# Moving the attention of a Macaron block against its mixture-of-experts passes, by a table of times

## The chip, the cores and the metric

The kernel runs on one NeuronCore of a Trainium2 chip. The metric is device time in microseconds (us), from the first to the last instruction of one launch. Engines: PE is TensorE, DVE is VectorE, ACT is ScalarE, POOL is GpSimd, SP is SyncE, which here only issues DMAs. Each engine works through its own instructions in a fixed order and waits on semaphores for the others.

## The reference

Eight batches (B) of 512 tokens (S) with 256 features (D) go through three sublayers:

```python
x = x + 0.5 * ffn(layernorm(x))          # "first" pass of the batch
x = x + attn(layernorm(x))               # RMS norm inside, 16 heads of 16, causal, output projection, + residual
x = x + 0.5 * ffn(layernorm(x))          # "second" pass of the batch

def ffn(x):                              # top-1 of E = 2 experts, FF = 1024
    probs = softmax(x @ gate_w.T); sel = argmax(probs); top_w = probs[sel]
    h = silu(x @ w_gate[sel].T) * (x @ w_up[sel].T)
    return (h @ w_down[sel].T) * top_w
```

`attn` is `softmax(mask(q k^T / 16)) v @ Wo + residual` with q, k, v from `rms_norm(x) * rms_w`.

## The kernel before, in words

**The FFN.** Tokens of one or two batches are sorted by expert into one array in DRAM (`x_sorted`) and processed in slots of 128 tokens. There are 12 passes (`PASSES`): 8 of one batch (5 slots) and 4 of two batches (9 slots), 76 slots in all. In a pass's first and last slot the expert is known when the program is built; in those between, the address of the weights is computed in registers (`expert[n, s]`, L1072 and L1080). A slot has two units (halves of FF). A unit is `gate` and `up` on PE (24 matmuls each, L1135 to L1137), `tanh` on ACT (L737), `hid` on DVE (L946, L950), the split into a high and a low part (`h_split`: L743 on ACT, L676 on POOL), and `down` on PE (12 matmuls, L1154 to L1156).

**The route of a batch** leads up to its pass: statistics on DVE (`l_stats`, L897), scale on POOL (L603 to L606), the normed rows on ACT (`l_norm`, L716; `l_split`, L724, which waits until the batch before has been scattered, L723), the low part on POOL (`l_low`, L610), the router's logits on DVE (`l_dlogit`), a count of places on PE (`l_prefix`, L1099 to L1104), the places on DVE (`l_pos`, L931), the scatter by four indirect DMAs from POOL (`l_scatter`, L624), and the transposed load from SP (`l_load`, L518) that the pass's first `gate` waits for (L1124). Behind a pass, POOL gathers the rows back (`y_gather`, L649, four indirect DMAs) and adds them to x (`x_update`, L631).

**Attention.** For each batch: `stats` on DVE (L957, waits for `x_update`), `rstd` on POOL, `norm` on ACT (L768), two `transpose` stages (PE L1169, ACT L778, DVE L975), `residual` on DVE, six projections (`proj`: PE L1060, then ACT L796 or L788, then DVE), and for q and k a store to DRAM (`qk_store`) from which SP reads the heads back in another layout (`qk_in`, eight DMAs a part). Then four parts of four heads (32 parts in all). A part has ten fills: `scores` on PE (L1197, L1199), `row_min` on DVE; later, from the row maxima on, `scores_t` on PE (L1214, L1216), `exp` on ACT (L814, L815), `p_lo` on DVE (L1029) for eight fills and on POOL (L681) for two, `pv` on PE (L1234), and `o_norm` on DVE. When the four parts are done come two transposes ("o") and two `out_proj`. `scores`, `scores_t`, transposes and projections take turns in three PSUM banks.

**What sets the order.** `master()` gives every stage a point on one common axis and sorts; every engine runs its share in that order. An FFN slot is 12 points and the passes stand at fixed points (`PASS_AT`, the last one ending at 925). Attention part p starts at `PART_AT + PART_POINTS * p`; a batch's norm, projections and loads stand at fixed distances ahead of its first part. A point has no fixed length: the engines take what time they need, and wait where the order lets them run into each other.

Of the kernel before, what the change touches and what calls it, by code (L numbers as in the profile page):

```python
# [33 lines left out]
GROUPS = 4  # L34
# [75 lines left out]
UNIT_POINTS = 6  # L110
SLOT_POINTS = 2 * UNIT_POINTS
PASS_AT = [SLOT_POINTS * at for at in SLOT_AT[:4]] + [336, 396, 462, 522, 630, 738, 798, 865]
PART_AT = 115
PART_POINTS = 21
FILL_POINTS = PART_POINTS / 10
LEAD = 33
PAIR_LAG = 9

NORM_AT = [-40, -39.5, -38.5, -36, -34, -32.4]
RESIDUAL_AT = -33  # L120
PROJ_AT = [-30.7, -28.2, -25.7, -23.2, -20.7, -18.2]
STORE_LAG = 1.0
QK_IN_AT = [-22, -16, -14, -14]
MAX_PARTS_AT = 21.5
ROW_MAX_AT = 24
SOFTMAX_AT = 31
# [5 lines left out]
COEF_LAG = 1.0  # L132
GATHER_LAG = 8
UPDATE_LAG = 16
OUT_AT = [122, 123.5, 125.5, 127.5]
ROUTE_STEPS = [("l_stats", 0, 0.0), ("l_stats", 1, 0.5), ("l_rstd", 0, 1.5), ("l_norm", 0, 4.0),
               ("l_split", 0, 6.0), ("l_dlogit", 0, 6.0), ("l_low", 0, 8.5), ("l_exp", 0, 10.5), ("l_prefix", 0, 11.0),
               ("l_pos", 0, 11.2), ("l_coef", 0, 13.0), ("l_scatter", 0, 14.5), ("l_load", 0, 19.0)]
# [9 lines left out]
def part_at(p, point):  # L148
    return PART_AT + PART_POINTS * p + point


def master():

    plan = []

    def put(at, *stage):
        plan.append((at, len(plan), stage))

    for u, (n, s, q) in enumerate(UNITS):
        p = PASS_AT[n] + SLOT_POINTS * s + UNIT_POINTS * q  # L160
        if s == 0 and q == 1:
            put(p, "flags", n)
            put(p + COEF_LAG, "coef", n)
        for kb in range(KB):
            put(p + kb, "gate", u, kb)
            put(p + 2 + kb, "up", u, kb)
            put(p + 10 + kb, "down", u, kb)
        put(p + 1 + TANH_LAG, "tanh", u)
        put(p + 3 + HID_LAG, "hid", u)
        put(p + 5.5, "h_split", u)  # L170
        if q:
            put(p + 11.3, "y_out", u // 2)
            put(p + 12.3, "y_store", u // 2)

    for k, (n, i, what, b) in enumerate(ITEMS):
        end = PASS_AT[n] + SLOT_POINTS * SLOTS[n] + 5.2 * i
        put(end + GATHER_LAG, "y_gather", k)
        at = end + UPDATE_LAG
        if what == "first":
            at = min(at, part_at(GROUPS * b, NORM_AT[0]) - 1)  # L180
        put(at, "x_update", k)
        at = PASS_AT[n] - LEAD - PAIR_LAG * (len(PASSES[n]) - 1 - i)
        if what == "second":
            at = max(at, part_at(GROUPS * b, OUT_AT[3] + 1))
        elif b >= 2:
            put(at - 8, "x_load", b)
        for stage, part, off in ROUTE_STEPS:
            if stage == "l_load":
                if i == len(PASSES[n]) - 1:
                    put(START_AT[stage, part] if n == 0 else at + off, stage, n)  # L190
            else:
                put(START_AT[stage, part] if n == 0 else at + off, stage, k, part)

    for w, at in enumerate(MAX_AT):
        put(at, "w_max", w)
    for k, at in enumerate(SCALE_AT):
        put(at, "w_scale", k)
    for w in range(PIECES):
        put(SPLIT_AT[w], "w_split", w)
    put(UNIT_POINTS * ONES_UNIT + 5.6, "ones")  # L200

    for b in range(B):
        first = GROUPS * b
        norm = [("stats", b, 0), ("stats", b, 1), ("rstd", b), ("norm", b), ("transpose", b, "attn", 0),
                ("transpose", b, "attn", 1)]
        for where, stage in zip(NORM_AT, norm):
            put(part_at(first, where), *stage)
        put(part_at(first, RESIDUAL_AT), "residual", b)
        for m in range(NP):
            put(part_at(first, PROJ_AT[m]), "proj", b, m)  # L210
            put(part_at(first, PROJ_AT[m] + STORE_LAG), "qk_store", b, m)
        out = [("transpose", b, "o", 0), ("transpose", b, "o", 1), ("out_proj", b, 0), ("out_proj", b, 1)]
        for where, stage in zip(OUT_AT, out):
            put(part_at(first, where), *stage)

    for p in range(PARTS):
        put(part_at(p, QK_IN_AT[p % GROUPS]), "qk_in", p)
        for f in range(FILLS):
            put(part_at(p, f * FILL_POINTS), "scores", p, f)
            put(part_at(p, f * FILL_POINTS) + ROW_MIN_LAG, "row_min", p, f)  # L220
            at = part_at(p, SOFTMAX_AT + (f + 0.5) * FILL_POINTS)
            put(at, "scores_t", p, f)
            put(at + EXP_LAG, "exp", p, f)
            put(at + FILL_POINTS, "p_lo", p, f)
            put(at + PV_LAG * FILL_POINTS - 0.2, "pv", p, f)
            if f % KINDS == KINDS - 1:
                put(at + PV_LAG * FILL_POINTS + 0.8, "o_norm", p, f // KINDS)
        put(part_at(p, MAX_PARTS_AT), "max_parts", p)
        put(part_at(p, ROW_MAX_AT), "row_max", p)

    return [stage for _, _, stage in sorted(plan)]
# [13 lines left out]
def macaron(nc, x, rms_w, gate_w, w_gate, w_up, w_down, w_attn, out):  # L245
    with ExitStack() as ctx:  # L246
# [1036 lines left out]
```

## Time and profile before

| | us |
|---|---|
| median of 3 runs (1254.82 to 1256.56) | 1255.71 |
| the profiled execution | 1255.95 |
| its span, first to last instruction | 1254.2 |

| engine | busy us | share |
|---|---|---|
| PE | 1078.9 | 86% |
| DVE | 860.2 | 69% |
| ACT | 744.7 | 59% |
| POOL | 571.8 | 46% |

PE's busy time is a union of pipelined matmuls. Idle time before an instruction is shown in brackets with what ended it.

### The profile page before, as it was taken

What the parts mean: (1) busy time and instruction counts of PE and PEld (TensorE: products, weight loads), DVE (VectorE), ACT (ScalarE), POOL (GpSimd) and SP (SyncE); (2) the same over time, 40 slices, a digit from 0 to 9 for tenths busy, and PEclk for the clock granted to TensorE, in tenths of its full rate; (3) what the DMA queues carried; (4) which work ended last, traced back from release to release, by engine and by line L of the source; (5) the groups of instructions that cost most, each with busy time, mean ns of one, the idle gap of its engine ahead of it and who ended that gap; (6) DMA issues with size and microseconds to landing.
All of it is one profiled execution on the core that took longest, in us unless ns stands there. A gap on an engine that the chain in (4) does not pass through costs nothing. (4 is left out here: it accounts for less than half of the span.)

```text
span 1254.2 us, 39207 instructions
## 1 busy us (share of the span) xinstructions
PE 1078.9 (86%) x14566; PEld 933.9 (74%) x14566; DVE 860.2 (69%) x1784; ACT 744.7 (59%) x1285; POOL 571.8 (46%) x693
## 2 busy tenths in 40 slices
PE   0677889986979989989998799998999999989894
PEld 0666778775868877778777678877777888778774
DVE  6643646785767886767787867888677797775421
ACT  3532525674757866666676667775766676776321
POOL 3146544344352344645354545334573255655443
PEclk9889889997989999989999899999999999999998
DMA  8203251212211122122223041112321112211211
GB/s 316 84 24 90 66 94 45 78 45 81 59 53 48 32 63 75 47 64 64 80 60 94 25 112 53 41 33 70 81 81 36 53 33 73 84 50 49 53 44 47
DMA packets 110670, 83.99 MB, mean 67 GB/s; under 512 B 59616, under 2 KB 104416, under 8 KB 110496
## 3 DMA queue, kind: packets, MB, share of 16 engines
q1 hardware_dynamic: 93408, 54.22, 15.7%
q0 software_dynamic: 6144, 17.31, 4.3%
q10 hardware_dynamic: 10944, 9.97, 2.5%
q8 instruction: 131, 2.15, 0.7%
q14 instruction: 43, 0.35, 0.1%
HBM read 37.26 MB, written 34.23 MB: 57 GB/s over the span
## 5 line engine op out<-in xcount | busy, mean ns | idle before, releaser
L676 POOL TENSOR_TENSOR h_lo<-hid,h_hi 128x256 bf16<-128x256 f32 x304 | 217.7, 737 | 480.9 <-ACT h_hi L743 479.9
L814 ACT ACTIVATE area<-ps_w,s_scale 128x512 f32<-128x512 f32 x320 | 219.4, 686 | 218.0 <-PE ps_w L1216 170.1
L1135 PE MATMUL ps_g<-x_t,w 128*128 128x128 f16 x1096 | 209.8, 226 | 15.5 <-issue 9.2
L1029 DVE TENSOR_TENSOR area<-area 128x512 f16<-128x512 f32 x256 | 206.6, 807 | 18.9 <-ACT area L815 15.4
L815 ACT ACTIVATE area<-ps_w,s_scale 128x512 f16<-128x512 f32 x320 | 218.0, 681 | 0.0
L1137 PE MATMUL ps_g<-x_t,w 128*128 128x128 f16 x1096 | 209.9, 226 | 2.0 <-issue 1.8
L1136 PE MATMUL ps_g<-x_t,w 128*128 128x128 f16 x1096 | 209.1, 225 | 1.8 <-issue 1.8
L1135 PE MATMUL ps_u<-x_t,w 128*128 128x128 f16 x1096 | 205.6, 222 | 2.9 <-issue 2.7
L1137 PE MATMUL ps_u<-x_t,w 128*128 128x128 f16 x1096 | 205.8, 222 | 1.7 <-issue 1.5
L1136 PE MATMUL ps_u<-x_t,w 128*128 128x128 f16 x1096 | 204.5, 221 | 1.8 <-issue 1.8
L1154 PE MATMUL ps_y<-wd,h_hi 128*128 (+1 forms) x608 | 169.1, 278 | 14.8 <-POOL h_lo L676 12.1
L1156 PE MATMUL ps_y<-wd,h_lo 128*128 (+1 forms) x608 | 169.2, 278 | 0.3 <-issue 0.3
L1155 PE MATMUL ps_y<-wd,h_hi 128*128 (+1 forms) x608 | 169.0, 278 | 0.1
L1197 PE MATMUL ps_w<-kt,qt 65*128 65x512 f16 (+3 forms) x512 | 138.2, 308 | 17.9 <-DVE row_min L1006 11.8
L1214 PE MATMUL ps_w<-qt,kt 67*128 67x512 f16 (+3 forms) x512 | 135.9, 304 | 17.4 <-DVE row_min L1008 7.3
L1135 PEld LDWEIGHTS ps_g<-x_t,w 128*128 (+1 forms) x1096 | 110.8, 101 | 33.0 <-issue 17.5
L737 ACT ACTIVATE hid<-ps_g,g_scale 128x512 f32<-128x512 f32 x137 | 94.3, 688 | 68.4 <-PE ps_g L1137 46.9
L1234 PEld LDWEIGHTS ps_v<-v_parts,area 128*128 128x128 f16 x2560 | 100.4, 97 | 37.3 <-POOL area L681 12.1
L1234 PE MATMUL ps_v<-v_parts,area 128*128 128x33 f16 x2560 | 115.8, 178 | 13.3 <-POOL area L681 10.2
L946 DVE SCALAR_TENSOR_TENSOR hid<-hid,ps_g 128x512 f32<-128x512 f32 x137 | 92.9, 678 | 48.4 <-ACT hid L737 48.3
L1006 DVE TENSOR_REDUCE row_min<-ps_w 128x1 f32<-128x512 f32 x128 | 87.6, 684 | 48.3 <-PE ps_w L1199 37.0
L1135 PEld LDWEIGHTS ps_u<-x_t,w 128*128 (+1 forms) x1096 | 107.9, 98 | 16.3 <-issue 6.3
(160 smaller groups left out, 2806.8 us busy)
## 6 DMA issues: line engine op xcount, KB each, us to landing
y_sorted<-ys ACTq DMA_DIRECT2D x76, 128.0 KB
qk_scratch<-area SPq DMA_DIRECT2D x32, 256.0 KB
qt<-qk_scratch SPq DMA_DIRECT2D x128, 64.0 KB, 2.7
kt<-qk_scratch SPq DMA_DIRECT2D x128, 64.0 KB, 2.8
x_buf<-x SPq DMA_DIRECT2D x8, 512.0 KB, 4.3
out<-x_buf SPq DMA_DIRECT2D x8, 512.0 KB, 2.9
x_sorted<-zeros SPq DMA_DIRECT2D x18, 136.0 KB, 2.0
area<-w_down SPq DMA_DIRECT2D x4, 512.0 KB, 12.8
```

Source lines behind the costliest of these rows:

```text
L676: pool.tensor_tensor(h_lo[:, u % 2, c], hid[:, u % 2, c], h_hi[:, u % 2, c], ALU.subtract).then_inc(h_lo_done, 1)
L814: act.activation(p_f32[:, f % 3], ps[:], ACT.Exp, scale=s_scale[:])
L815: act.activation(p_hi[:, f % 4], ps[:], ACT.Exp, scale=s_scale[:]).then_inc(exp_done, 1)
L1029: dve.tensor_tensor(p_lo[:, f % 4], p_f32[:, f % 3], p_hi[:, f % 4], ALU.subtract).then_inc(lo_done, 1)
L1135: pe.matmul(cols, w_hi, x_hi, start=kb == 0 and f == 0, stop=False, skip_group_check=True)
L1136: pe.matmul(cols, w_hi, x_lo, start=False, stop=False, skip_group_check=True)
L1137: ins = pe.matmul(cols, gate_up(u, kind, 1, kb, q * QF + f), x_hi, start=False, stop=kb == KB - 1, skip_group_check=True)
L1154: pe.matmul(ps_y[:, 0:D], hi, wd_lo, start=q == 0 and f == 0, stop=False, skip_group_check=True)
L1155: pe.matmul(ps_y[:, 0:D], hi, wd_hi, start=False, stop=False, skip_group_check=True)
L1156: ins = pe.matmul(ps_y[:, 0:D], lo, wd_hi, start=False, stop=q == 1 and f == QF - 1, skip_group_check=True)
L1197: pe.matmul(ps[:, at:at + keys], qt[0:MAX_AT_ROW, h, i * P:keys], kt[0:MAX_AT_ROW, h, 0:keys], start=n == 0, stop=False, skip_group_check= ...
L1234: ins = pe.matmul(ps_o[n // KINDS % 2][:, hh, i, :], part[:, n % 4, at + (i - j) * P:at + (i - j + 1) * P], v_parts[b % 2][:, j, h, :], st ...
```

## The change

It alters numbers in the table. `PART_AT` goes from 115 to 97 and `PART_POINTS` from 21 to 21.3: part 0 starts 18 points earlier, part 31 8.7 points earlier (766 becomes 757.3). For batches 0 and 2 (`AT_ONCE`) norm, residual, projections and the first load have tables of their own, about half as wide: from the statistics to the last projection 12.3 points in place of 21.8. `OUT_AT` moves 2.5 points away from the last part. The same instructions run; only their order changes. `x_update` of batches 0 and 2 stands two points later (76 and 244). The FFN's points do not move.

```diff
-PART_AT = 115
-PART_POINTS = 21
+PART_AT = 97
+PART_POINTS = 21.3
...
+NORM0_AT = [-20, -19.8, -19.4, -18.4, -17, -16]
+RESIDUAL0_AT = -13
+PROJ0_AT = [-15.2, -13.7, -12.2, -10.7, -9.2, -7.7]
+QK_IN0_AT = -12
+AT_ONCE = (0, 2)
...
-OUT_AT = [122, 123.5, 125.5, 127.5]
+OUT_AT = [124.5, 126, 128, 130]
...
-            at = min(at, part_at(GROUPS * b, NORM_AT[0]) - 1)
+            at = min(at, part_at(GROUPS * b, NORM_AT[0] if b not in AT_ONCE else NORM0_AT[0]) - 0.5)
...
-        for where, stage in zip(NORM_AT, norm):
+        for where, stage in zip(NORM_AT if b not in AT_ONCE else NORM0_AT, norm):
             put(part_at(first, where), *stage)
...
-            put(part_at(first, PROJ_AT[m]), "proj", b, m)
-            put(part_at(first, PROJ_AT[m] + STORE_LAG), "qk_store", b, m)
+            at = part_at(first, (PROJ_AT if b not in AT_ONCE else PROJ0_AT)[m])
+            put(at, "proj", b, m)
+            put(at + STORE_LAG, "qk_store", b, m)
...
-        put(part_at(p, QK_IN_AT[p % GROUPS]), "qk_in", p)
+        put(part_at(p, QK_IN0_AT if p in (0, 2 * GROUPS) else QK_IN_AT[p % GROUPS]), "qk_in", p)
```

The changed program has seven more lines, so a stage's line number there is 7 higher behind the tables.

**ACT, batch 0 beside the routes of batches 2 and 3 (points 88 to 96).** `e_abs` is the router's exponential of batch 2, `v_parts` and `area<-ps_w` are projections (v, and q or k), `xs_rows` is `l_split` of batch 3, `h_hi` and `hid` are the FFN's. Before:

```order
L728 ACTIVATE e_abs<-neg_abs 128x4
L751 ACTIVATE ys<-ps_y,coef 128x256
L788 ACTIVATE v_parts<-ps_w 128x32x16
L743 ACTIVATE h_hi<-hid 128x512
L759 DMA y_sorted<-ys 128x256
L737 ACTIVATE hid<-ps_v,g_scale 128x512
L716 ACTIVATE xn_f<-x_buf,l_shift,l_scale 128x256 x4
L788 ACTIVATE v_parts<-ps_w 128x32x16
L724 ACTIVATE xs_rows<-xn_f 128x4x256
L796 ACTIVATE area<-ps_w 128x512
L743 ACTIVATE h_hi<-hid 128x512
L796 ACTIVATE area<-ps_w 128x512
```

The same place now:

```order
L735 ACTIVATE e_abs<-neg_abs 128x4
L758 ACTIVATE ys<-ps_y,coef 128x256
L803 ACTIVATE area<-ps_w 128x512
L750 ACTIVATE h_hi<-hid 128x512
L766 DMA y_sorted<-ys 128x256
L744 ACTIVATE hid<-ps_v,g_scale 128x512
L723 ACTIVATE xn_f<-x_buf,l_shift,l_scale 128x256 x4
L731 ACTIVATE xs_rows<-xn_f 128x4x256
L750 ACTIVATE h_hi<-hid 128x512
L744 ACTIVATE hid<-ps_g,g_scale 128x512
```

Both v projections and the first of the last two now stand ahead of this stretch, the last one near its start, and `l_split` is followed by the FFN's `h_hi` at once.

**POOL, around the scatter of pass 5 (points 371 to 380).** `x_sorted` is the scatter, `area<-area` is the `p_lo` of every fifth fill, `h_lo` the FFN's low part. Before:

```order
L610 TENSOR_TENSOR xs_rows<-xn_f,xs_rows 128x4x256
L676 TENSOR_TENSOR h_lo<-hid,h_hi 128x256 x2
L624 DMA x_sorted<-xs_rows,place 1152x272 x4
L681 TENSOR_TENSOR area<-area 128x512
L676 TENSOR_TENSOR h_lo<-hid,h_hi 128x256 x2
L681 TENSOR_TENSOR area<-area 128x512
```

Now:

```order
L617 TENSOR_TENSOR xs_rows<-xn_f,xs_rows 128x4x256
L688 TENSOR_TENSOR area<-area 128x512
L683 TENSOR_TENSOR h_lo<-hid,h_hi 128x256 x2
L631 DMA x_sorted<-xs_rows,place 1152x272 x4
L683 TENSOR_TENSOR h_lo<-hid,h_hi 128x256 x2
L688 TENSOR_TENSOR area<-area 128x512
L683 TENSOR_TENSOR h_lo<-hid,h_hi 128x256 x2
L688 TENSOR_TENSOR area<-area 128x512
```

The `p_lo` that stood right behind the four scatter DMAs has moved ahead of them, and the next one stands further behind.

**DVE, the statistics of batch 2 (points 241 to 246 before, 244 to 250 now).** `bn<-x_buf` is `stats`, which waits for `x_update`. Before:

```order
L1023 TENSOR_SCALAR max_parts<-row_min 128x16
L1024 SCALAR_TENSOR_TENSOR max_parts<-row_min,max_parts 128x16
L1050 TENSOR_TENSOR x_buf<-ps_w,x_buf 128x512
L946 SCALAR_TENSOR_TENSOR hid<-hid,ps_g 128x512
L950 SCALAR_TENSOR_TENSOR hid<-hid,ps_u 128x512
L957 BN_STATS bn<-x_buf 128x6 x2
L1006 TENSOR_REDUCE row_min<-ps_w 128x1
L957 BN_STATS bn<-x_buf 128x6 x2
L961 BN_AGGR mean_var<-bn 128x2 x4
```

Now:

```order
L1010 TENSOR_REDUCE row_min<-ps_w 128x2
L1020 TENSOR_REDUCE row_min<-row_min 128x4
L1036 TENSOR_TENSOR area<-area 128x512
L1013 TENSOR_REDUCE row_min<-ps_w 128x1
L1030 TENSOR_SCALAR max_parts<-row_min 128x16
L1031 SCALAR_TENSOR_TENSOR max_parts<-row_min,max_parts 128x16
L964 BN_STATS bn<-x_buf 128x6 x4
L968 BN_AGGR mean_var<-bn 128x2 x4
L1013 TENSOR_REDUCE row_min<-ps_w 128x1
```

The statistics stood between `row_min` of two fills right behind an output projection of batch 0 (`x_buf<-ps_w`); that projection is long over now, and they stand in one piece, further behind their `x_update`.

## Rows read from the trace of the kernel before

**Rows 1.** The page, part 1: busy time, share of the span, instructions.

```profile
PE 1078.9 (86%) x14566; PEld 933.9 (74%) x14566; DVE 860.2 (69%) x1784; ACT 744.7 (59%) x1285; POOL 571.8 (46%) x693
```

**Rows 2.** Stretches: busy time (count) of PE, PEld, DVE, ACT, POOL; clock; DMA.

```profile
100.00:180.00 80.00, 63.39 (x716) 54.76 (x714) 35.41 (x89) 28.88 (x51) 45.61 (x56) 0.90 0.36 84
...
370.00:1150.00 780.00, 718.67 (x10068) 620.78 (x10066) 604.38 (x1233) 534.28 (x931) 363.25 (x418) 0.98 0.21 61
```

**Rows 3.** Timeline of PE near the third pass: start, length, idle before, releaser.

```profile
127.63 1.08 PE L1169 MATMUL ps_w<-ident,area 128*128 128x128 f32 x4 [4.82 <-ACT area L768]
...
155.46 0.28 PE L1154 MATMUL ps_y<-wd,h_hi 128*128 x1 [1.78 <-POOL h_lo L676]
...
176.16 0.29 PE L1135 MATMUL ps_g<-x_t,w 128*128 128x128 f16 x1 [3.67 <-DMA x_t<-x_sorted]
```

**Rows 4.** Stretches just behind waits of PE (clock is the seventh column).

```profile
309.00:313.00 4.00, 4.00 (x34) 3.29 (x35) 3.45 (x8) 1.78 (x3) 1.08 (x2) 0.50 0.66 143
...
155.40:158.90 3.50, 3.44 (x39) 2.86 (x39) 2.81 (x7) 1.44 (x5) 3.48 (x4) 1.00 0.55 187
...
176.10:182.00 5.90, 5.84 (x57) 5.65 (x58) 1.40 (x3) 0.69 (x1) 0.00 (x0) 0.56 0.41 49
```

**Rows 5.** Timelines of POOL, DVE and ACT: the norm of batch 0.

```profile
118.87 2.36 POOL L631 TENSOR_TENSOR x_buf<-yt,x_buf 128x1024 f32<-128x1024 f32 x1 [0.53 <-DMA yt<-y_sorted,place]
...
121.27 1.40 DVE L957 BATCH_NORM_STATS2 bn<-x_buf 128x6 f32<-128x256 f32 x4 [1.05 <-POOL x_buf L631]
...
125.41 2.07 ACT L768 ACTIVATE area<-x_buf,shifts,scales 128x256 f32<-128x256 f32 x4 [3.76 <-POOL shifts L661]
```

**Rows 6.** Timeline of PE at a count of places; one projection (L1060 alone).

```profile
139.97 0.17 PE L1099 MATMUL ps_w<-sel,upper 128*128 128x5 bf16 x1
...
140.10:141.60 1.50, 1.50 (x12) 1.45 (x12) 1.00 0.77 253
```

**Rows 7.** Timelines of ACT and SP before the third pass.

```profile
152.50 1.06 ACT L724 ACTIVATE xs_rows<-xn_f 128x1024 f16<-128x1024 f32 x1 [5.35 <-DMA x_sorted<-xs_rows,place]
...
165.79 4.31 SPq L518 DMA_TRANSPOSE x_t<-x_sorted  x1
```

**Rows 8.** One fill of scores on PE; group of DVE on the page.

```profile
207.12:207.47 0.35, 0.35 (x8) 0.28 (x6) 0.00 (x0) 0.35 (x2) 0.00 (x0) 1.00 0.00 0
...
L1029 DVE TENSOR_TENSOR area<-area 128x512 f16<-128x512 f32 x256 | 206.6, 807 | 18.9 <-ACT area L815 15.4
```

**Rows 9.** Stretches of one unit each, in the last pass.

```profile
1206.50:1210.50 4.00, 4.00 (x50) 3.27 (x48) 0.69 (x1) 0.77 (x2) 1.30 (x2) 1.00 0.00 0
...
1228.20:1230.85 2.65, 2.65 (x50) 2.64 (x49) 0.37 (x1) 0.78 (x2) 1.30 (x2) 1.00 0.03 6
```

**Rows 10.** Timeline of PE: six waits in the middle and late part.

```profile
308.97 0.41 PE L1234 MATMUL ps_v<-v_parts,area 128*128 128x33 f16 x8 [3.42 <-POOL area L681]
...
355.44 0.29 PE L1197 MATMUL ps_w<-kt,qt 65*128 65x128 f16 x1 [5.60 <-DVE row_min L1006]
...
362.16 0.41 PE L1169 MATMUL ps_w<-ident,area 128*128 128x128 f32 x2 [0.61 <-ACT area L768]
...
552.82 0.34 PE L1234 MATMUL ps_v<-v_parts,area 128*128 128x33 f16 x7 [3.57 <-POOL area L681]
...
699.55 0.52 PE L1169 MATMUL ps_w<-ident,o_buf 128*128 128x128 f32 x3 [4.13 <-DVE o_buf L1044]
...
1141.42 0.24 PE L1234 MATMUL ps_v<-v_parts,area 128*128 128x33 f16 x3 [2.27 <-POOL area L681]
```

**Rows 11.** Timelines of POOL and DVE before three of those waits.

```profile
307.75 1.16 POOL L681 TENSOR_TENSOR area<-area 128x512 f16<-128x512 f32 x1
...
354.05 0.75 DVE L957 BATCH_NORM_STATS2 bn<-x_buf 128x6 f32<-128x256 f32 x2 [5.17 <-POOL x_buf L631]
...
695.96 2.12 POOL L610 TENSOR_TENSOR xs_rows<-xn_f,xs_rows 128x1024 f16<-128x1024 f32 x1
...
696.55 2.08 DVE L1029 TENSOR_TENSOR area<-area 128x512 f16<-128x512 f32 x1
```

More of the change, by code:

```diff
@@ L205, in master @@
                 ("transpose", b, "attn", 1)]
-        for where, stage in zip(NORM_AT, norm):
+        for where, stage in zip(NORM_AT if b not in AT_ONCE else NORM0_AT, norm):
             put(part_at(first, where), *stage)
-        put(part_at(first, RESIDUAL_AT), "residual", b)
+        put(part_at(first, RESIDUAL_AT if b not in AT_ONCE else RESIDUAL0_AT), "residual", b)
         for m in range(NP):
-            put(part_at(first, PROJ_AT[m]), "proj", b, m)
-            put(part_at(first, PROJ_AT[m] + STORE_LAG), "qk_store", b, m)
+            at = part_at(first, (PROJ_AT if b not in AT_ONCE else PROJ0_AT)[m])
+            put(at, "proj", b, m)
+            put(at + STORE_LAG, "qk_store", b, m)
         out = [("transpose", b, "o", 0), ("transpose", b, "o", 1), ("out_proj", b, 0), ("out_proj", b, 1)]
```

## The prediction

> **What bounds the kernel.** I read the busy shares first: PE works 1078.9 of 1254.2 us [rows 1], so 175 us are its idle time. Then the stretches: from 370 to 1150 us PE is busy 718.7 of 780 us (92%); from 100 to 180 us, the second pass with the norm and projections of batch 0, it is busy 63.4 of 80 us at a mean clock of 0.90 [rows 2]. The change adds and removes no work on PE. It can only change when PE waits, what a wait does to its clock, and what runs beside what. So the third view is PE's timeline, searched for waits, and the fourth the timelines of the engines that end them.
>
> Two prices first. The longer waits cost more than themselves: behind the 3.42 us at 308.97 the clock is 0.50 for the next 4 us, the 1.2 GHz level, while behind the 1.78 us at 155.46 it stays 1.00 [rows 3, 4, 10]. PE's work of 4 us at half speed is 2 us at full speed, so such a wait costs 2 us on top; I take 1.7, since in some of them PE is not at its limit, and I charge it to waits of about 3.4 us and more. And the middle slots of a pass, with addresses from registers, run slower when nothing stands between their matmuls: 50 matmuls take 4.00 us in a middle slot of the last pass and 2.65 us in its last slot [rows 9], 1.35 us a unit, 2.7 a slot.
>
> **Step 1, the norm of batch 0: +2.5 us.** Its chain is timed by data: `x_update` at 118.87 (2.36 us), statistics at 121.27 (1.40), norm at 125.41 (2.07), and PE's first transpose at 127.63 after a wait of 4.82 us [rows 3, 5]. Pressing it into fewer points makes none of it faster. PE arrives one point earlier (transposes at 80 in place of 81), one half of a `gate` or `up`, 12 of the 50 matmuls above: 0.7 us more wait. Second, transpose and first projection had a `down` half and a `gate` half between them and now have next to nothing, while ACT and DVE must write the high and low part of x, 512 columns each: 1.0 us by half of ACT's 2.07 for 1024 columns [rows 5], 0.8 us by DVE's mean for 512 [rows 8]. Sum 2.5 us. Bounds: 0.7 and 4.
>
> **Step 2, the route of batches 2 and 3: +4.5 us.** Projections now stand ahead of the count of places at point 89 that ran at 139.97: five instead of two. One costs 1.50 us [rows 6], so the count comes 4.5 us later measured by what PE has done, and with it places, scatter and the ACT instruction that waits for this scatter. That one (L724, 152.50) sat 5.35 us [rows 7], with the FFN's `h_hi` queued behind it; PE paid only 1.78 us since the last projections lay there as cover. Now they stand earlier: no cover is left, but part of the delay is work that PE has done. I take 2.8 of the 4.5 us as showing: 4.6 us of wait in place of 1.78, now with the clock's price, so 2.8 + 1.7 = 4.5. Bounds: 0 if the other engines have slack there, and 4.5 + 1.7 = 6.2.
>
> **Step 3, the gate of the third pass: -3.6 us.** PE waits 3.67 us for the transposed load at 176.16 and then runs 5.90 us at 0.56 [rows 3, 4]. The load went out at 165.79 [rows 7]. Between points 97 and 120 there are now eight more `scores` fills, 0.35 us each [rows 8], 2.8 us of work that fills the wait; against that the load is later by step 2. I take the wait as 2.2 us, below what costs the clock: 1.5 + 2.1 (5.9 us at 0.56 is 2.6 lost, of which I keep 0.5). Bounds: -5.8, and +1.2 if the load slips by as much as the count does. On SP the second part's loads (eight issues) now stand ahead of this load; they stand well ahead of the moment when the scatter lets it go, so I price them at nothing; at worst they hold SP as long as the load's own issue does, 4.31 us [rows 7].
>
> **Step 4, middle slots: -1.4 and +1.8 us.** At points 97 to 108 a middle slot now has `scores` between its units (-1.4, half a slot's 2.7). At the other end the attention's last `pv` comes 8.1 points sooner (814.9, was 823.0), which leaves 8.1 of 12 points of a middle slot bare: 2.7 x 0.68 = 1.8. The last pass is not waiting for batch 7 in either order: its route stands at point 832 in both.
>
> **Step 5, batch 2: -1.2 us.** DVE waited 5.17 us for `x_update` ahead of a `row_min` (354.05), and PE 5.60 us at 355.44 and 0.61 at 362.16 [rows 10, 11]. `x_update` is timed by the gathers ahead of it on POOL, so it won't come sooner; the statistics stand 4.4 points further back, so DVE no longer blocks. But from statistics to transpose there are 3 points in place of 6, about 3.5 us of PE's work at the mixed rate (1255 us for the 985 points from -60 to 925, 1.2 to 1.3 us a point), for a chain that took 8 us (354.05 to 362.16). The wait moves to the transpose, about 5 us, the clock's price stays.
>
> **Step 6, POOL's `p_lo` behind indirect DMAs: -7.6 us.** The `p_lo` behind four scatter DMAs runs at 307.75, and `pv` waits 3.42 us for it [rows 10, 11]. The same stands ahead of 552.82 (3.57) and, behind a gather, 1141.42 (2.27). By the points, `p_lo` stood 0.5 to 0.6 behind a scatter three times and 0.3 behind a gather once. Parts at 21.3 points move the distances: only one is now under 2 points behind a scatter or a gather (0.8, behind the gather at 746). Gone: 3.42 + 1.7 + 3.57 + 1.7 + 2.27 = 12.7; new: 3.4 + 1.7 = 5.1.
>
> **Step 7, the output of batch 3: -5.8 us.** PE's transpose waited 4.13 us at 699.55 for `o_norm`, late on DVE behind a `p_lo` of 2.08 us that met POOL's 2.12 us `l_low` [rows 10, 11]. It is now 12 points ahead of these routes, and 2.2 points behind `o_norm` instead of 0.9: 4.13 + 1.7.
> The rule for such a meeting is in the Trainium skill, "SBUF — State Buffer", section Who interferes with whom: DVE and POOL share one pair of ports that one instruction holds to its end, so the other waits. The trace agrees: DVE's instruction ends 0.5 us after POOL's and takes 2.08 us where its group's mean is 0.81 [rows 8, 11]. By the rule the change cannot remove such meetings, since nearly all of the 16 `l_low` and 16 `x_update` still lie beside attention; it moves them. Each is then 1.3 us on DVE somewhere else, and by it alone step 7 would be nothing.
>
> **Sum.** 2.5 + 4.5 - 3.6 - 1.4 + 1.8 - 1.2 - 7.6 - 5.8 = -10.8 us. I don't believe all of it. Steps 6 and 7 list waits that I see vanish; those that new coincidences will make I can't see, and PE idles 61 us from 370 to 1150 us [rows 2], far more than the waits I have named there. I give back half: -5.4. From 1255.95 us (span 1254.2 and 1.75 around it; 0.24 above the median) this is 1250.5.
>
> **The rivals.**
> *Slower: the route gives way at the head.* If the scatter of batch 2 slips by the full 4.5 us, step 2 costs 6.2, and the load of the third pass is late as well (+1.2): with step 1 +9.9 us at the third pass, and -1.4 + 1.8 - 1.2 leaves +9.1. It decides once new waits in the middle eat a third of steps 6 and 7 (13.4 us); at two thirds the time is 1256 + 9.1 - 4.5 = 1260.6. For it: ACT has an instruction there that already sat 5.35 us. Against: the projections that delay the route are off PE sooner.
> *No change.* The vanished waits come back elsewhere all but a few us, which pay for the head (2.5 + 4.5 - 3.6 = 3.4): 1256. For it: every fixed length of POOL's blocks (2.12 us of `l_low`, four DMAs a scatter) still meets attention [rows 11], and all fixed distances inside a batch are the same. Against: the nearest `p_lo` distances are plainly better.
> *The list holds.* No new waits: 1255.95 - 10.8 = 1245. For it: attention's parts are 1.4% further apart. Against: the idle 61 us, which have a cause at each place, and all places move.
>
> **How the numbers follow.** Forecast 0.43; the list holds 0.18; no change 0.14; slower 0.25. Range: 1240 to 1261. The low end is 5 us under the full list, where steps 2 and 3 at their low bounds would put it 6.7 under; the high end is the slower case. The forecast's own range is 1246 to 1254. A measurement here tells 0.2%, 2.5 us, from no change. Faster by more (below 1253.2): 0.18, 0.38 of the forecast's and 0.02 of no change's, 0.58; within: 0.05, 0.08 and 0.01 of the slower case's, 0.14; slower by more: 0.24 and 0.04 of no change's, 0.28.
>
> **What the profile will show.** Step 1: PE's wait at L1176 for batch 0 of 5 to 6 us, and one of 1 to 2 us ahead of its first L1067. Step 2: a wait of PE on `h_lo` around 155 to 162 us of 4 to 5 us at a low clock behind it. Step 3: the wait for the load of the third pass between 1 and 3 us. Step 5: DVE's wait for `x_update` of batch 2 gone, PE's at the transpose about 5. Step 6: PE's waits at L1241 on POOL together under 6 us (10.2 before), at most one over 3. Step 7: no wait over 2 us at an output transpose. The tail from the last `exp` on is 1 to 2 us longer. The forecast is wrong if the sum of PE's idle time falls by less than 3 us or more than 15, or if the difference at the start of the third pass is beyond 0 to +6 us.

## The result, and the profile after

The changed kernel is slower: 1271.66 us (4 runs, 1270.83 to 1272.07) beside 1256.13 for the kernel before on the same chip, ratio 1.0122 with a 95% interval of 1.0093 to 1.0151. A second job gave 1270.6 beside 1254.82, again 1.0122 (1.0096 to 1.0149). The forecast was 1250.5 and its range ended at 1261. The profiled execution took 1271.53 us, its span 1269.8.

The page of the changed kernel, part 1 and three groups of part 5 (busy us, mean ns, idle us before them and what ended most of it):

```profile
PE 1093.3 (86%) x14566; PEld 944.5 (74%) x14566; DVE 864.2 (68%) x1784; ACT 743.6 (59%) x1285; POOL 571.6 (45%) x693
...
L1221 PE MATMUL ps_w<-qt,kt 67*128 67x512 f16 (+3 forms) x512 | 137.9, 308 | 25.9 <-DVE row_min L1015 11.7
L1204 PE MATMUL ps_w<-kt,qt 65*128 65x512 f16 (+3 forms) x512 | 136.8, 305 | 10.5 <-DVE row_min L1013 4.0
...
L1241 PE MATMUL ps_v<-v_parts,area 128*128 128x33 f16 x2560 | 117.5, 179 | 9.3 <-POOL area L688 4.5
```

Set against [rows 1]: the same 14566 matmuls keep PE busy for 14.4 us more, while its idle time, span less busy, is 176.5 us where it was 175.3. Over the whole of this execution, then, the loss shows as slower matmuls and not as more waiting. The sum hides two things, which the stretches below bring out: the head has less idle time and the middle more. Within the idle time `scores_t` (L1221) waits much more, `pv` (L1241) and `scores` (L1204) less. The same three groups of the kernel before:

```profile
L1197 PE MATMUL ps_w<-kt,qt 65*128 65x512 f16 (+3 forms) x512 | 138.2, 308 | 17.9 <-DVE row_min L1006 11.8
L1214 PE MATMUL ps_w<-qt,kt 67*128 67x512 f16 (+3 forms) x512 | 135.9, 304 | 17.4 <-DVE row_min L1008 7.3
...
L1234 PE MATMUL ps_v<-v_parts,area 128*128 128x33 f16 x2560 | 115.8, 178 | 13.3 <-POOL area L681 10.2
```

The three groups together wait 45.7 us after and 48.6 before, so it is the distribution that changed, not the sum.

Where in the program? Stretches of the changed kernel (busy and count of PE, PEld, DVE, ACT, POOL; clock; DMA), then one of the kernel before that [rows 2] doesn't have, and last the middle of the changed kernel in its second job:

```profile
0.00:370.00 370.00, 285.04 (x3583) 245.01 (x3584) 233.13 (x507) 189.55 (x320) 168.23 (x222) 0.92 0.30 87
100.00:180.00 80.00, 62.13 (x704) 53.62 (x704) 40.28 (x97) 27.82 (x49) 43.85 (x54) 0.89 0.32 84
370.00:1150.00 780.00, 711.97 (x9741) 615.41 (x9740) 592.92 (x1203) 516.35 (x901) 348.65 (x404) 0.96 0.21 59
```
```profile
0.00:370.00 370.00, 278.41 (x3488) 242.28 (x3489) 225.04 (x489) 181.56 (x306) 165.89 (x221) 0.93 0.30 87
```
```profile
370.00:1150.00 780.00, 709.40 (x9814) 612.51 (x9815) 594.57 (x1213) 520.88 (x910) 354.42 (x410) 0.98 0.21 59
```

The number to read is the count in brackets behind PE's busy time: how many matmuls start in a stretch of equal length. In the first 370 us the changed kernel does 95 more (3583 for 3488); at the 9.4 matmuls a us of that stretch it is some 10 us ahead (13 us if each matmul is weighed by its columns, by my estimate). From 370 to 1150 us it does 327 fewer (9741 for 10068, 12.9 a us): 25 us lost. The head, about which the forecast's slower rival spoke, gains; the long middle loses. PE's idle time says the same once it is taken by stretch: 85.0 us in the head where it was 91.6, 68.0 in the middle where it was 61.3.

The second job's profile warns against reading too much into the clock. There the middle has 254 matmuls fewer than before at the same mean clock of 0.98, and 70.6 us idle. Over its whole span of 1266.0 us PE is busy for 1085.5: 6.6 us more busy and 5.2 us more idle than before. The loss is the same; how it divides into slower matmuls and waiting is not.

The middle once more by line, changed kernel (first job), then before. The group of `gate` tells of the clock, since its work and shape are the same:

```profile
L1142 PE MATMUL ps_g<-x_t,w 128*128 128x128 f16 x726 | 140.8, 227 | 0.8 <-issue 0.3 <-DVE hid L953 0.2
...
L1221 PE MATMUL ps_w<-qt,kt 67*128 67x384 f16 (+3 forms) x414 | 111.3, 307 | 23.0 <-DVE row_min L1015 11.7 <-DVE row_min L1010 6.4 <-DVE xt_lo L982 3.2
```
```profile
L1135 PE MATMUL ps_g<-x_t,w 128*128 128x128 f16 x749 | 139.4, 222 | 1.7 <-DVE hid L946 1.6
...
L1214 PE MATMUL ps_w<-qt,kt 67*128 67x512 f16 (+3 forms) x431 | 113.4, 302 | 10.6 <-DVE row_min L1008 6.3 <-DVE row_min L1003 1.2 <-ACT area L815 1.0
```

A `gate` matmul takes 227 ns where it took 222, 2% more at a mean clock of 0.96 for 0.98. And the wait of `scores_t` has more than doubled, 23.0 us for 10.6, most of it for `row_min`.

One such wait in full, changed kernel, PE and then DVE (start, length, idle before):

```profile
872.82 0.27 PE L1204 MATMUL ps_w<-kt,qt 65*128 65x256 f16 x1
...
874.83 0.36 PE L1241 MATMUL ps_v<-v_parts,area 128*128 128x33 f16 x8
875.04 0.38 PE L1204 MATMUL ps_w<-kt,qt 65*128 65x512 f16 x1
875.25 0.22 PE L1206 MATMUL ps_w<-mask_s,ident 128*128 128x128 bf16 x1
879.10 0.61 PE L1221 MATMUL ps_w<-qt,kt 67*128 67x512 f16 x1 [3.63 <-DVE row_min L1010]
```
```profile
872.76 0.42 DVE L916 CUSTOM_DVE_ANT_0 junk<-xn_f,w_diff 128x256 bf16<-128x256 f32 x1
...
875.37 1.97 DVE L924 TENSOR_SCALAR sel<-dlogit 128x4 bf16<-128x4 f32 x1
...
877.32 1.11 DVE L927 SCALAR_TENSOR_TENSOR neg_abs<-dlogit 128x4 f32<-128x4 f32 x1
878.36 0.68 DVE L1010 TENSOR_REDUCE row_min<-ps_w 128x2 f32<-128x512 f32 x1
```

DVE works on a route's logits until 878.4. The `row_min` of the fill that PE wrote at 872.82 stands behind them. Three banks take turns, so the `scores_t` that follows the next `scores` needs just that bank. It stands right behind that `scores` (875.04), with `pv` ahead of both. PE works in order, so all that stands behind this `scores_t` waits with it.

**Why they stand so.** The diff doesn't name it: `FILL_POINTS` is `PART_POINTS / 10`, so it goes from 2.1 to 2.13, while `SOFTMAX_AT` stays 31 points. The softmax side starts 14.76 fills behind the part's first `scores` before, 14.55 now. With the half fill that the code adds, `scores_t` stood 0.55 of a point behind a `scores` and `pv` 0.35 behind it; now `scores_t` stands 0.115 behind and `pv` 0.085 ahead. That holds in all 320 fills. Between a `scores` and the `scores_t` that takes its bank lie 2.24 points instead of 2.65. The other way round, from a `scores_t` to the `scores` that takes its bank, there are 4.14 instead of 3.65, which fits that `scores` waits less now.

### The profile page after: what moved, and what is told of

It is laid out like the page before. It is cut to its first block and busy times, and to the rows that moved or that the text cites. A ratio compares the mean times of both kernels' runs of the same rounds, so it can differ in the third digit from the quotient of the medians.

```text
span 1269.8 us, 39207 instructions
## 1 busy us (share of the span) xinstructions
PE 1093.3 (86%) x14566; PEld 944.5 (74%) x14566; DVE 864.2 (68%) x1784; ACT 743.6 (59%) x1285; POOL 571.6 (45%) x693
## 3 DMA queue, kind: packets, MB, share of 16 engines
q1 hardware_dynamic: 93408, 54.22, 15.5%
## 5 line engine op out<-in xcount | busy, mean ns | idle before, releaser
L683 POOL TENSOR_TENSOR h_lo<-hid,h_hi 128x256 bf16<-128x256 f32 x304 | 220.7, 747 | 515.6 <-ACT h_hi L750 515.0
L1142 PE MATMUL ps_g<-x_t,w 128*128 128x128 f16 x1096 | 212.4, 227 | 14.1 <-issue 9.4
L1144 PE MATMUL ps_g<-x_t,w 128*128 128x128 f16 x1096 | 213.0, 227 | 1.0 <-issue 1.0
L1143 PE MATMUL ps_g<-x_t,w 128*128 128x128 f16 x1096 | 211.7, 226 | 1.1 <-issue 1.0
L1142 PE MATMUL ps_u<-x_t,w 128*128 128x128 f16 x1096 | 208.0, 224 | 4.5 <-issue 4.3
L1144 PE MATMUL ps_u<-x_t,w 128*128 128x128 f16 x1096 | 208.0, 224 | 1.4 <-issue 1.4
L1143 PE MATMUL ps_u<-x_t,w 128*128 128x128 f16 x1096 | 206.8, 223 | 1.2 <-issue 1.2
L1036 DVE TENSOR_TENSOR area<-area 128x512 f16<-128x512 f32 x256 | 197.4, 771 | 7.4 <-ACT area L822 5.1
L1161 PE MATMUL ps_y<-wd,h_hi 128*128 (+1 forms) x608 | 170.2, 280 | 14.4 <-POOL h_lo L683 12.3
L1221 PE MATMUL ps_w<-qt,kt 67*128 67x512 f16 (+3 forms) x512 | 137.9, 308 | 25.9 <-DVE row_min L1015 11.7
L1204 PE MATMUL ps_w<-kt,qt 65*128 65x512 f16 (+3 forms) x512 | 136.8, 305 | 10.5 <-DVE row_min L1013 4.0
L1241 PE MATMUL ps_v<-v_parts,area 128*128 128x33 f16 x2560 | 117.5, 179 | 9.3 <-POOL area L688 4.5
L1015 DVE TENSOR_REDUCE row_min<-ps_w 128x4 f32<-128x512 f32 x128 | 87.8, 686 | 44.2 <-PE ps_w L1206 33.3
```

Source lines behind the costliest of these rows:

```text
L683: pool.tensor_tensor(h_lo[:, u % 2, c], hid[:, u % 2, c], h_hi[:, u % 2, c], ALU.subtract).then_inc(h_lo_done, 1)
L1036: dve.tensor_tensor(p_lo[:, f % 4], p_f32[:, f % 3], p_hi[:, f % 4], ALU.subtract).then_inc(lo_done, 1)
L1142: pe.matmul(cols, w_hi, x_hi, start=kb == 0 and f == 0, stop=False, skip_group_check=True)
L1143: pe.matmul(cols, w_hi, x_lo, start=False, stop=False, skip_group_check=True)
L1144: ins = pe.matmul(cols, gate_up(u, kind, 1, kb, q * QF + f), x_hi, start=False, stop=kb == KB - 1, skip_group_check=True)
L1161: pe.matmul(ps_y[:, 0:D], hi, wd_lo, start=q == 0 and f == 0, stop=False, skip_group_check=True)
```

## The experiments

Ratios are to the kernel before on the same chip, with their 95% intervals. In each job several kernels shared its runs. "D" edits the changed kernel, "B" the kernel before.

**The pressed tables alone.** D: attention's start, spacing and output back.

```diff
-PART_AT = 97
-PART_POINTS = 21.3
-OUT_AT = [124.5, 126, 128, 130]
+PART_AT = 115
+PART_POINTS = 21
+OUT_AT = [122, 123.5, 125.5, 127.5]
```

> The pressed tables for batches 0 and 2 alone: attention still starts at point 115, parts 21 apart, outputs at their old points; nothing else differs from before. Theory A (the pressed norm and projections cost, as steps 1 and 2 of the prediction have it): slower than before by 5 to 10 us. Theory B (the loss comes from how the parts, now 21.3 points apart, meet the FFN's fixed points from batch 3 on; the pressed tables cost little): within 4 us of before, 1252 to 1260.

Measured: 1260.88, ratio 1.0039 (1.001 to 1.0068). The tables cost some 5 us (1.3 to 8.5 by the interval), about a third of the loss and the low edge of theory A; the rest comes with start and spacing.

**Spacing 21 with the early start.** D: `PART_POINTS = 21`, which also restores the order in a fill (`SOFTMAX_AT` is again 14.76 fills).

> The changed kernel with the parts 21 points apart again (start at 97, pressed tables, later outputs kept). Theory A: the head is the same, so it stays at 1266 to 1272. Theory B (spacing): the loss of 15.5 us goes with the spacing; 1247 to 1256. Theory C (any shift of attention against the FFN's points makes other collisions, and this one drew bad ones): some third value, not closer to 1256 than to 1272 by rule.

Measured: 1279.8, ratio 1.0181 (1.014 to 1.0222): slower still. So the wider spacing by itself is not what costs, and the old order in a fill does not by itself make the early start fast.

**The order in a fill put back.** D: `SOFTMAX_AT = 31.45`, 0.565 and 0.365 of a point behind `scores` again.

> The changed kernel with SOFTMAX_AT 31.45 in place of 31: inside a fill PE's order is again scores, pv, scores_t with FFN work between, as before the change, where the changed kernel has pv, scores, scores_t back to back; all else keeps its place within half a point. Theory D (the back-to-back pair makes PE wait for row_min and exp a little in every fill, which costs the clock): at least half of the 15.5 us comes back, 1256 to 1264. Theories A and B: 1268 to 1274.

Measured: 1257.65, ratio 1.0018 (0.9991 to 1.0045). One number gives back some 13 of the 15.5 us, by the two ratios.

**The same loss made in the kernel before.** B: `SOFTMAX_AT = 30.55`, `scores_t` 0.1 behind, `pv` 0.1 ahead.

> The kernel before with SOFTMAX_AT 30.55 in place of 31: inside a fill PE's order becomes pv, scores, scores_t back to back, as in the changed kernel; start, spacing and tables stay as before. Theory D: slower by 8 us or more, 1264 to 1272. Theories A and B: within 4 us of before.

Measured: 1272.13, ratio 1.0125 (1.0084 to 1.0166), the whole of the change's loss with start, spacing and tables as they were. The stretch from 370 to 1150 us, first with the order put back, then with it broken in the kernel before:

```profile
370.00:1150.00 780.00, 716.20 (x9903) 621.28 (x9902) 594.33 (x1213) 523.17 (x912) 361.77 (x415) 0.96 0.21 60
```
```profile
370.00:1150.00 780.00, 717.42 (x9868) 618.10 (x9865) 602.04 (x1222) 526.65 (x915) 347.00 (x407) 0.96 0.21 59
```

162 matmuls more than after in the one, 200 fewer than before in the other. So 0.45 of a point between the softmax side (`scores_t`, `exp`, `p_lo`, `pv`) and the rest is shown as the cause of most of the loss: taken back in one table and made in another, it moves the time by 1.0% and 1.25%. That it works through the order inside a fill is not shown by these two, since the same edit also moves the softmax side of all 320 fills by 0.45 of a point against the FFN, whose points are fixed.

**`pv` alone, `scores_t` alone.** D, the first: `pv` 0.45 later (0.365 behind `scores`). The second: `scores_t` back, `pv` held ahead.

```diff
-            put(at + PV_LAG * FILL_POINTS - 0.2, "pv", p, f)
+            put(at + PV_LAG * FILL_POINTS + 0.25, "pv", p, f)
```
```diff
-SOFTMAX_AT = 31
+SOFTMAX_AT = 31.45
...
-            put(at + PV_LAG * FILL_POINTS - 0.2, "pv", p, f)
+            put(at + PV_LAG * FILL_POINTS - 0.65, "pv", p, f)
```

> The kernel after with pv alone put back behind scores in every fill (0.36 of a point behind it, as before); scores_t stays 0.11 behind scores. Pair theory (what costs is scores and scores_t of one fill standing back to back, so that the ACT and DVE work on each meets): the loss stays, 1268 to 1274 us. Pv theory (what costs is pv standing ahead of scores): the loss goes, 1255 to 1260. If pv between the two is itself enough to part them, and both matter alike: 1262 to 1266. The order scores, scores_t, pv is new here, so the pair theory has its own risk of 3 us either way.

> The kernel after with scores_t alone put back (0.56 of a point behind scores, as before); pv stays 0.09 ahead of scores. Pair theory: 1255 to 1260 us, as with both put back (1257.65). Pv theory: 1268 to 1274.

Measured: 1260.9, ratio 1.0016 (0.9988 to 1.0044), and 1267.8, ratio 1.0087 (1.0052 to 1.0122). The pair theory fails: `scores_t` right behind `scores` is harmless once `pv` is later. This also says how little the long waits shown above are worth. With `pv` later the loss is gone within what can be told, and yet `scores_t` in the middle still waits 20.3 us, most of it for `row_min`, where it was 23.0 in the changed kernel and 10.6 before:

```profile
L1221 PE MATMUL ps_w<-qt,kt 67*128 67x384 f16 (+3 forms) x420 | 112.0, 305 | 20.3 <-DVE row_min L1010 7.9 <-DVE row_min L1015 6.8 <-DVE xt_lo L982 3.2
```

But the second edit also took 0.45 of a point from the time between `p_lo` and `pv`, and the first gave as much to it. So place and slack had to be parted:

**`pv` later, its slack held.** D: as the first, and `p_lo` 0.45 later too.

> The kernel after with pv 0.45 of a point later, as in the run with pv alone put back (1260.9 us), and with p_lo 0.45 later as well, so that pv has no more time behind its p_lo than before. Place theory (pv standing ahead of scores is what costs): the loss stays away, 1256 to 1263. Slack theory (what helped was the time from p_lo to pv, 4.06 points made 4.51, and pv's place in the fill counts for nothing): the loss is back, 1267 to 1273, with PE's waits at L1241 for POOL's p_lo at 5 us or more in all (none over 1 us in the run with pv alone).

Measured: 1272.72, ratio 1.0111 (1.0066 to 1.0155). The loss is back with PE's order `scores`, `scores_t`, `pv` unchanged, so `pv`'s place among the others counts for nothing that can be told here. The order in which PE takes the three stages of a fill is thus not the cause by itself. PE's waits, first of the run with `pv` later, then with `p_lo` later too (us in total, times, longest):

```profile
PE ps_w L1221 <- DVE row_min L1010: 9.3, 7, 3.6
...
PE ps_w L1221 <- DVE row_min L1015: 6.8, 8, 1.6
```
```profile
PE ps_w L1221 <- DVE row_min L1010: 8.1, 5, 3.6
...
PE ps_w L1221 <- DVE row_min L1015: 6.5, 8, 1.6
PE ps_w L1204 <- DVE row_min L1013: 6.3, 3, 3.9
...
PE ps_w L1221 <- DVE row_min L1013: 4.8, 5, 2.6
...
PE ps_v L1241 <- POOL area L688: 3.5, 3, 2.5
```

I expected 5 us or more for POOL's `p_lo`; it is 3.5, and none in the other. As much of the difference is in the waits for `row_min`, which shares DVE with four `p_lo` of five. I didn't find which of the two weighs more.

**More room in the kernel before.** B: the softmax side 0.3 later; `pv` 0.45 later; both.

```diff
-SOFTMAX_AT = 31
+SOFTMAX_AT = 31.3
```

> The kernel before with SOFTMAX_AT 31.3 in place of 31: scores_t 0.85 of a point behind scores (was 0.55), pv 0.65 (was 0.35). If the distance counts evenly, one that is wider by 0.3 gives back some of what 0.45 less took (16 us): 1246 to 1253. If only standing back to back costs: 1254 to 1259. If any move of the softmax against the FFN's fixed points costs or gives by chance: outside 1250 to 1262 on either side with no link to the distance.

> The kernel before with pv 0.45 of a point later (0.80 behind scores, scores_t at 0.55). Slack theory: PE's waits at L1234 for POOL's p_lo (10.2 us in all, three of them over 3 us) go nearly all, with the clock behind them: 1256 less 8 to 14, so 1242 to 1249. Place theory: pv is behind scores in both, so no gain, 1253 to 1259.

> The kernel before with the softmax side 0.3 of a point later (1254.18 us alone, 0.9963 of before) and pv 0.45 later still. Slack theory: both gains add up as far as they are not the same waits; the softmax step left 10.1 us at L1234, so 1240 to 1248. Place theory: as with 0.3 alone, 1251 to 1258.

Measured: 1254.18, ratio 0.9963 (0.9935 to 0.9992); 1257.71, ratio 0.9988 (0.9964 to 1.0012); 1253.82, ratio 0.9957 (0.9935 to 0.9978). A softmax side 0.3 later gains 0.4%, in line with the distance from `scores` to `scores_t`, though like the runs above it also moves against the FFN. The slack of `pv` gives no gain that can be told from none, though it took the waits for POOL's `p_lo` from 10.2 to 6.7 us: of the 8 to 14 us expected of it, at most 4.5 are inside the interval. In the changed kernel the same 0.45 gave back 1%.

The last one was run again on another chip:

> The kernel before with the softmax side 0.3 later and pv 0.45 later still, unchanged from the run at 0.9957. If that was the order's: 0.993 to 0.998. If it was the chip's: 0.999 to 1.003.

Measured: 1249.36 beside 1254.82, ratio 0.9953 (0.9935 to 0.9972). It beats the kernel before on two chips, and the changed kernel, at 1270.6, in this job.

**Other starts.** D with the order in a fill put back, begun at 99 in place of 97:

```diff
-PART_AT = 97
-SOFTMAX_AT = 31
+PART_AT = 99
+SOFTMAX_AT = 31.45
```

> The kernel after with the old order in a fill (SOFTMAX_AT 31.45) and attention begun at 99 in place of 97, all else the same. If the order in a fill is what counts, this stays at 1257.65 within 4 us (1254 to 1262). If it is how attention's fills meet the FFN's routes and gathers that counts, 2 points shift every one of these meetings by nearly a whole fill, and the time leaves that band, as 97 with a spacing of 21 points did (1279.8): over 1264, or under 1252.

Measured: 1284.12, ratio 1.0195 (1.0165 to 1.0224). Two points of start, 22 us by the ratios (1.0018 at 97). This shift leaves all distances inside attention alone, so it is attention's place against the FFN that costs here, more than the whole change did. Which of the meetings costs was not found; the next runs test one kind. It also means that the softmax side's move against the FFN stands as a rival to its distance from `scores` in the runs above. For the distance speaks that 0.45 of a point was worth about the same in two tables whose meetings with the FFN differ; no run parts the two.

**Is it POOL's `p_lo` behind indirect DMAs?** With spacing 21 and start 97, seven of them stand 0.35 to 1.05 points behind a scatter or a gather (four in the kernel before, one in the changed one). Timelines of that kernel, POOL and then PE:

```profile
906.27 0.99 POOL L631 DMA_INDIRECT x_sorted<-xs_rows,place  x1 [0.15 <-issue]
907.56 0.96 POOL L631 DMA_INDIRECT x_sorted<-xs_rows,place  x1 [0.30 <-issue]
908.83 0.96 POOL L631 DMA_INDIRECT x_sorted<-xs_rows,place  x1 [0.30 <-issue]
910.10 0.96 POOL L631 DMA_INDIRECT x_sorted<-xs_rows,place  x1 [0.30 <-issue]
911.09 1.16 POOL L688 TENSOR_TENSOR area<-area 128x512 f16<-128x512 f32 x1
```
```profile
912.31 0.27 PE L1241 MATMUL ps_v<-v_parts,area 128*128 128x33 f16 x4 [3.42 <-POOL area L688]
```

Four DMAs hold POOL for 4.8 us (906.27 to 911.06), and `pv` waits. First cure: `pv` 0.45 later in this kernel (D with `PART_POINTS = 21` and the `pv` edit above). Second: POOL's `p_lo` ahead of the DMAs.

```diff
-            put(at + FILL_POINTS, "p_lo", p, f)
+            put(at + FILL_POINTS - (0.7 if f % KINDS == KINDS - 1 else 0), "p_lo", p, f)
```

> The kernel after with parts 21 points apart (1279.8 us) and pv 0.45 of a point later. That kernel has six waits at L1241 for POOL's p_lo, 22.2 us in all, four or five long enough to bring the clock down. Slack theory: most of them go, and with them 15 to 25 us: 1256 to 1265. If the spread between starts (97, 99, 115) is not from p_lo behind the indirect DMAs but from FFN and attention meeting on DVE and ACT: 1272 to 1280.

> The kernel after with parts 21 points apart (1279.8 us) and POOL's p_lo 0.7 of a point sooner, one fill in five; it then stands ahead of six of the seven blocks of indirect DMAs that it stood behind by 0.35 to 1.05 points. If these make up what this start and spacing lose: PE's 22.2 us of waits at L1241 for POOL fall under 6 and the time by 16 us and the clock behind five waits (1.7 each), to 1253 to 1262. If they are only part of it: 1265 to 1273. If they don't matter: 1276 to 1282.

Measured: 1285.19, ratio 1.0194 (1.0142 to 1.0245), slower than either forecast, and 1.0127 (1.009 to 1.0165; 1251.78 us on a chip where the kernel before took 1236.5). Later `pv` left 15.8 of 22.2 us of these waits and gained nothing. Moving `p_lo` left 8.4 us of them and the ratio is lower by 0.5%. So POOL's `p_lo` may be a part of it, on the assumption that a ratio carries from chip to chip, and not the bulk.

**The same edit on the kernel before and on the changed one.** B with 0.7; B with `SOFTMAX_AT = 31.3` and 1.0; D with 0.9.

> The kernel before with POOL's p_lo 0.7 of a point sooner: the three that stand 0.55 behind a scatter and the one 0.35 behind a gather come ahead of them. By step 6 of the prediction, 12.7 us less: 1242 to 1246. If other waits take their place: 1249 to 1256.

> The kernel before with the softmax side 0.3 later (0.9963 of before by itself) and POOL's p_lo 1.0 sooner, which brings the same four ahead of the DMAs. If both add: 1237 to 1245. If they overlap: 1246 to 1254.

> The kernel after with POOL's p_lo 0.9 of a point sooner and nothing else changed. If what later pv gave (11 us) was the 4.5 us of waits for POOL's p_lo and their clock: 1260 to 1265. If the time from p_lo to pv matters on all fills, DVE's four in five too, or the loss is scores_t waiting for the bank that row_min reads: 1267 to 1273.

Measured, all on that faster chip: 1.0029 (1.0007 to 1.0051), 1.0006 (0.9982 to 1.0029) and 1.0067 (1.0044 to 1.009). The first is step 6 of the prediction made by itself in the kernel before, and it gains nothing. The second shows no gain either: the 0.4% of the wider distance (0.9963, on another chip) is not seen with it. Two of PE's waits in the first:

```profile
PE ps_w L1060 <- DVE xt_lo L975: 15.7, 7, 2.6
...
PE ps_v L1234 <- POOL area L681: 2.8, 1, 2.8
```

The waits for POOL fell from 10.2 to 2.8 us, as meant. Other waits are longer there: those of the projections for `xt_lo` are 15.7 us and those of `down` for `h_lo` 17.6, where the trace of before has 6.0 and 12.1 on its own chip. In the changed kernel the edit took 0.5% off (1.0122 to 1.0067, again across chips), though its waits for POOL's `p_lo` were 4.5 us and are 6.0; I have no explanation for that one.

**The changed kernel again**, to see whether its ratio depends on the chip:

> The kernel after, unchanged, once more beside before. If the ratio is a property of the order: 1.0093 to 1.0151 again, whatever before takes in this job. If it depends on the chip: a ratio near 1.007 where before takes some 1237 us.

Measured: 1.0122 (1.0096 to 1.0149), told at the start. The chip of that job wasn't the fast one, so whether ratios differ there stays open.

## Why the prediction was wrong, step by step

The changed kernel's PE timeline at the places of the steps:

```profile
127.06 1.09 PE L1176 MATMUL ps_w<-ident,area 128*128 128x128 f32 x4 [5.92 <-ACT area L775]
131.80 0.47 PE L1067 MATMUL ps_w<-xt_hi,wa_hi 128*128 128x512 f32 x1 [1.70 <-issue]
150.81 0.28 PE L1161 MATMUL ps_y<-wd,h_hi 128*128 x1 [1.53 <-POOL h_lo L683]
160.62 0.39 PE L1161 MATMUL ps_y<-wd,h_hi 128*128 x1 [1.61 <-POOL h_lo L683]
181.65 0.23 PE L1142 MATMUL ps_g<-x_t,w 128*128 128x128 f16 x1 [2.02 <-DMA x_t<-x_sorted]
363.50 0.87 PE L1176 MATMUL ps_w<-ident,area 128*128 128x128 f32 x3 [3.78 <-ACT area L775]
...
1087.93 0.37 PE L1241 MATMUL ps_v<-v_parts,area 128*128 128x33 f16 x8 [3.26 <-POOL area L688]
```

and three of its stretches, for the clock:

```profile
161.00:166.00 5.00, 5.00 (x53) 4.12 (x51) 3.32 (x7) 1.60 (x3) 3.57 (x5) 0.71 0.08 26
181.70:187.00 5.30, 5.30 (x74) 4.74 (x75) 2.91 (x5) 0.84 (x2) 0.00 (x0) 1.00 0.02 5
...
600.80:604.20 3.40, 3.40 (x33) 2.85 (x33) 2.40 (x3) 1.71 (x4) 2.00 (x3) 0.50 0.23 77
```

- Step 1 held. 5.92 and 1.70 us against 4.82 [rows 3]: +2.8, forecast +2.5. The profile puts the 1.70 down to `issue`, but in DVE's timeline `xt_lo` (130.95, 0.74 us) ends 0.11 us before that matmul, as the step has it.
- Step 2 was wrong in form: not one wait of 4 to 5 us but two of about 1.6, 1.4 us more than before. Yet the clock behind them is 0.71, where it stayed at 1.00 [rows 4].
- Step 3 held: 2.02 us, forecast 2.2, and the clock behind it is 1.00 instead of 0.56.
- Step 4 was not tested by itself. The tail from the last `exp` is not 1 to 2 us longer but 6 (113.4 us for 107.5): that `exp` stands 8.4 points sooner (816.95 to 808.54; the last `pv` 8.3, not the 8.1 of the step), and my line on the tail had left out that those points of FFN are now behind it.
- Step 5: 3.78 us in place of 5.60 and 0.61 [rows 10], so -2.4 before any clock, forecast -1.2. DVE no longer waits for `x_update` there.
- Step 6: the waits for POOL at L1241 are 4.5 us in all, one of them over 3, as forecast (under 6, at most one over 3; 10.2 before). In the second job's profile they are 8.3 us, one over 3, so the forecast sum does not hold in every execution. What such a wait is worth was wrong: taken away by themselves in the kernel before, they gave nothing (1.0029), and the `pv` edit gave 0.9988. I had entered 12.7 us for them.
- Step 7: the 4.13 us at an output transpose are gone. Nothing shows that the time fell by it. The prediction also worked out, from the shared port pair of DVE and POOL in the Trainium skill ("SBUF — State Buffer", Who interferes with whom), that such meetings would only move. DVE's times fit that: its `p_lo` instructions take 9.3 us less in all (206.7 to 197.4), its `max_parts` instructions 11.6 us more (18.8 to 30.4; 25.3 in the second job).

Steps 1 to 5 sum to +2.6 us in the forecast, and by 370 us the changed kernel is not behind but ahead: they are not where the loss is. **The step that failed is the sum's**: "I give back half", together with the rival's sentence that "all fixed distances inside a batch are the same". They were not. The spacing enters every fill through `FILL_POINTS`, and against a constant in points it moved the softmax side of all 320 fills by 0.43 of a point against `scores`, so that `pv` now stands ahead of `scores` and `scores_t` right behind it. This move was priced at nothing, and it costs some 13 us (put back: 1.0122 to 1.0018; made alone: 1.0125), more than the 10.8 us that the whole list was to gain. I compared the two orders at the places of the steps and never inside an ordinary fill, all 320 of which had changed. It can't be read in the diff's lines, but it can be worked out from them: 31 / 2.1 against 31 / 2.13.

The slower rival had the sign but not the place: it put the loss at the head. With the softmax side put back, start, spacing and tables give 1.0018 together, no change within what can be told, and the pressed tables cost 1.0039 of it; so start and spacing by themselves are worth some 0.2%, less than these intervals can tell.

The profile's sign of being wrong was there too: PE's idle time was to fall by 3 us or more, and it rose by 1.2 us in the first job's profile and by 5.2 in the second's.

The second fault was the price of the clock. I charged 1.7 us to waits of 3.4 us and more, and there are 9 such waits after and 10 before. But at 600.80 the clock is 0.50 with no wait longer than 2.02 us in the 10 us before. In the first job's profile the time at 0.50 is 132 us in 23 stretches (95 us in 17 before), far more stretches than waits of that length; in the second's it is 104 us at the same ratio. So the clock is a part of the loss whose size varies, and not its cause.

What stays open: by which mechanism the 0.43 of a point costs, through the waits inside a fill or through new meetings with the FFN. Two edits remove the loss, the whole softmax side later or `pv` alone later, and the second leaves most of the waits of `scores_t` in place. Open too is why two points of start cost 22 us.

## What to carry to other kernels

When a table of times is stretched, look for every number that is scaled by it and every one that is not, and compare order and distances inside the stage that repeats most, not only at the places where waits were seen. A wait seen on the critical engine can be worth less than its length, since other waits may grow when it goes: take it away by itself before it enters a sum. To judge two orders, count the matmuls that start in equal stretches, and take idle time by stretch as well: over the whole program a gain in one stretch hides a loss in another. Before a reading of idle time against clock is believed, look at a second execution.

## What the runs showed of the hardware

The 1.2 GHz level (clock 0.50) came here without a long wait. PE, changed kernel, ahead of the stretch at 600.80 with clock 0.50, and the 10 us before it, in which the clock was 1.00 and PE idle for 3.24 us, almost all in these two waits:

```profile
592.49 0.63 PE L1176 MATMUL ps_w<-ident,area 128*128 128x128 f32 x4 [1.21 <-ACT area L775]
...
599.33 0.47 PE L1067 MATMUL ps_w<-xt_hi,wa_hi 128*128 128x512 f32 x1 [2.02 <-DVE xt_lo L982]
```
```profile
590.80:600.80 10.00, 6.76 (x77) 5.45 (x73) 6.37 (x12) 5.92 (x11) 6.91 (x8) 1.00 0.29 81
```

The Trainium skill, "TensorE: Matmul & The Clock Gate", section A second HAM failure mode: psum-queue depth-cycling, tells of a kernel in which many short pauses of PE between groups of matmuls switched the clock to and fro. The rows above agree in one point, that pauses of 1.21 and 2.02 us came before the low level and no long one did; they show two pauses and not many.

How the loss is shared between idle time and clock varies: the changed kernel had a mean clock of 0.949 in one profile and 0.960 in the other, at spans of 1269.8 and 1266.0 us, with the same ratio of medians to before. Within one job, too, its four executions had mean clocks of 0.949 to 0.957 at spans of 1269.1 to 1270.3.

Chips differ by more than most edits: the kernel before took 1236.5 us (22 runs) in one job and 1254.8 to 1259.2 in five others. Only kernels of one job can be compared in us. The profiles of the fast job have one thing in common. A `gate` line of the kernel before, then the same line of B with `p_lo` ahead, from that job:

```profile
L1137 PE MATMUL ps_g<-x_t,w 128*128 128x128 f16 x1096 | 209.9, 226 | 2.0 <-issue 1.8
```
```profile
L1137 PE MATMUL ps_g<-x_t,w 128*128 128x128 f16 x1096 | 208.8, 226 | 0.0
```

The small pauses of PE that the profile puts down to `issue`, where it shows nothing that PE waits for, are missing. Behind the first 100 us they sum to 15 to 32 us in 34 to 58 pieces in the sixteen profiles of the other jobs, and to 0.6 to 1.9 us in one or two pieces in the four profiles of this one. That is about the size of the difference, 18 to 23 us; that it is the cause, and what makes the pauses, no run shows.
